# Attention scores over 128 contraction rows, rows cleared by a transfer, and new orders for every engine

## The chip, the cores and the metric

The kernel runs on one core of a Trainium2 chip. The metric is device time of one execution in microseconds (us), taken as the median of repeated runs. Five engines work side by side: PE (TensorE, matrix products), ACT (ScalarE), DVE (VectorE), POOL (GpSimd) and SP (SyncE, which here only issues DMA transfers). They wait for each other through semaphores. SBUF is the on-chip memory with 128 partitions (rows), PSUM holds the results of PE in 8 banks.

## What is computed

Cross attention with 16 heads of 32 columns over 32 batches of 512 queries and 512 keys. The reference, cut to what matters:

```
qn  = layer_norm(q, q_norm_g, q_norm_b);  kvn = layer_norm(kv, kv_norm_g, kv_norm_b)
Q, K, V = (qn @ Wq), (kvn @ Wk), (kvn @ Wv)        # each (32, 512, 512), then 16 heads of 32
scores = einsum('bhqd,bhkd->bhqk', Q, K) / sqrt(32)
attn   = softmax(scores)
ctx    = einsum('bhqk,bhkd->bhqd', attn, V)        # back to (32, 512, 512)
out    = q + gelu(ctx @ Wo + bo)
```

## The kernel before

**Tiling.** The work of a batch is cut into four units, one for each group of four heads (HU = 4, NU = 4); 32 batches give 128 units. Batches 1 to 30 run in one hardware loop, the others are written out. A batch is four steps of each engine's program. In step s the engine does, mixed with each other: the transposed scores, the exponentials and the context of unit s; the plain scores and their maxima of unit s+1; and the projections q and k of unit s+2. So each unit is computed two steps ahead.

**Kinds of work on PE**, by the letters of the ORDER table: `q`, `k`, `v`, `o` are projections, 12 products of 512 columns each, of which one table item issues two (line 856); `x` transposes one token tile (4 short matmuls, line 943); `s` is one plain score product whose row maximum DVE takes (line 883, reader: line 706); `st` is one transposed score product whose exponential ACT takes (line 876, reader: line 563); `pv` is half of a unit's context, 16 narrow matmuls (line 903); `z` sums the probabilities (line 847); `m` transposes the collected maxima (line 965). The two kinds of scores share four PSUM banks in the order in which they are issued.

**The stacks.** A number is kept as a high and a low part. To multiply both at once, the parts of q and k of one unit are stacked over the 128 rows: q_stack and k_stack have two slots each (even and odd units). Rows 0 to 95 hold q high, q high, q low against k high, k low, k high. Rows 96 to 127 of q_stack hold the shift (minus the maximum) that ACT writes once the maxima of the unit are known (line 617); the same rows of k_stack hold constants. The transposed scores contract over all 128 rows, the plain scores, which are needed before a shift exists, over 96 (KROWS).

**How a stack is filled.** ACT writes the high part of a projection, DVE the low part (line 688), and then SP issues three DMAs for q (table item `rq`) and three for k (`rk`), each 256 KB, out of the natural layout into 32 partitions of the stack (`restack`, line 353). Before them SP waits for two things: that the projection has left PSUM, and `stack_used`, which PE raises in the first `pv` that stands behind the last `st` of the step (AFTER_ST), because the unit that is now finished used the same slot. The first `s` of the new unit, in the next step, waits for q_stacked and k_stacked: all six transfers. SP issues everything through one queue, in the order of its table; it also issues the loads of token tiles (`load`), of the residual (`res`, `first_res`) and the stores.

**What sets the order.** Five tables (ORDER), one per engine, each with a string per step. Nothing is scheduled at run time but by semaphores.

Of the kernel before, what the change touches and what calls it, by code (L numbers as in the profile page):

```python
# [9 lines left out]
F32 = mybir.dt.float32  # L10
# [50 lines left out]
    ),  # L61
    "act": (
# [4 lines left out]
    ),  # L67
    "dve": (
# [4 lines left out]
    ),  # L73
    "pool": (
        "ln*3 split add*6 res_add ln*3",
        "ln*2 add*5 res_add add res_add split res_add",
        "split add*6",
        "add split add*5",
    ),
    "sp": (  # L80
        "load*8 rq rk store res",
        "rq rk store res store",
        "store first_res rk rq first_res",
        "rq rk",
# [94 lines left out]
def build(nc, x, ctx_in, q_g, q_b, kv_g, kv_b, wq, wk, wv, wo, bo, out):  # L179
    B = x.shape[0]  # L180
    with ExitStack() as es:
# [6 lines left out]
        def sem(name):  # L188
            return es.enter_context(nc.semaphore(name))
# [58 lines left out]
        stack_used = sem("stack_used")  # L248
        q_stacked = sem("q_stacked")
# [130 lines left out]
        def _(sp):  # L380
            def prepare(b, s):

                if (b, s) == (-1, 1):
# [18 lines left out]
            def batch(b):  # L402
                PLAN = plan_of(b)
                for s in range(NU):
# [4 lines left out]
                    for kind, n, part in PLAN["sp"][s]:  # L409
                        if kind == "load" and valid(b + 1):  # L410
                            load_tile(b + 1, n)
# [580 lines left out]
```

## Time and profile before

| | |
|---|---|
| median of 3 runs | 3265.43 us (3265.21 to 3265.64) |
| the profiled execution | 3262.8 us |
| span of its instructions | 3261.0 us |
| mean granted TensorE clock | 0.998 of full speed |
| PE busy | 99% of the span, 97% of the chain that ended last |
| DVE, ACT, POOL busy | 69%, 70%, 71% |
| DMA engines, mean busy share | 0.6, 105 GB/s |

How to read it: the span is what the records cover; some 2 us lie around it. The chain of work that ended last is followed back from the last instruction; its pieces begin where the piece before ends. Matmuls overlap, so the spacing between their starts, not their durations, is what PE costs.

### The profile page before, as it was taken

To read this page: it belongs to the slowest core of one execution; us is meant where nothing else is said; L and a number is where in the kernel's file an instruction comes from. 1 tells how busy PE (TensorE), PEld (TensorE's weight loads), DVE (VectorE), ACT (ScalarE), POOL (GpSimd) and SP (SyncE) were. 2 spreads that over 40 slices of the span, in tenths; PEclk is the share of its full clock that TensorE was granted. 3 is DMA by queue.
4 is the path that set the end of the run, shared out by engine and by line. 5 is a ranking of instruction groups with operands and counts; after the bars stand their busy time and mean duration, and the time that the engine had idled before them with its cause. 6 is when DMAs were issued, how large, how long until landed. Compare 5 with 4: busy or idle time off the path is not lost.

```text
span 3261.0 us, 49855 instructions
## 1 busy us (share of the span) xinstructions
PE 3230.8 (99%) x16611; PEld 2135.1 (65%) x16611; DVE 2256.9 (69%) x4769; ACT 2280.3 (70%) x3985; POOL 2313.9 (71%) x1544
## 2 busy tenths in 40 slices
PE   8999999999999999999999999999999999999998
PEld 5566666666666666666666666666666666666664
DVE  6667667676676676666766766766667767667664
ACT  5677666777767777667767667776777676677765
POOL 3676776777677767777776677777767776777765
PEclk9999999999999999999999999999999999999999
DMA  5655656566556656565665566665656655666653
GB/s 142 87 108 107 108 104 116 91 111 107 107 104 104 111 107 107 104 118 89 111 109 106 105 102 111 109 104 104 120 86 112 107 107 107 100 111 108 105 79 76
DMA packets 186721, 343.02 MB, mean 105 GB/s; under 512 B 20561, under 2 KB 20577, under 8 KB 186466
## 3 DMA queue, kind: packets, MB, share of 16 engines
q1 hardware_dynamic: 186000, 339.03, 60.0%
q8 instruction: 134, 2.20, 0.3%
q10 hardware_dynamic: 466, 0.80, 0.2%
q14 instruction: 121, 0.99, 0.1%
HBM read 104.87 MB, written 33.55 MB: 42 GB/s over the span
## 4 chain that ended last, share of the span: by engine, by line
PE 97%; DVE 1%; ACT 1%; issue 1%; DMA 0%; POOL 0%; SPq 0%; ACTq 0%; POOLq 0%; DVEq 0%
PE gen L856 43%; PE score L883 16%; PE score L876 15%; PE ctx L903 14%; PE gen L847 4%; PE gen L943 4%; PE gen L965 1%; DVE maxes L706 1%; DMA k_stack<-k_nat 0%; ACT q_stack L617 0%; PE score L788 0%; ACT probs L563 0%; DVE stats L725 0%; PE gen L837 0%; POOL probs L475 0%
## 5 line engine op out<-in xcount | busy, mean ns | idle before, releaser
L475 POOL TENSOR_TENSOR probs<-probs 128x1024 f32<-128x1024 f32 x762 | 1800.3, 2392 | 287.8 <-PE ctx L903 281.6
L706 DVE TENSOR_REDUCE maxes<-score 128x1 f32<-128x512 f32 x2048 | 1294.9, 680 | 217.5 <-PE score L883 213.9
L563 ACT ACTIVATE probs<-score 128x512 f32<-128x512 f32 x2048 | 1090.2, 621 | 141.1 <-PE score L876 137.5
L883 PE MATMUL score<-k_stack,q_stack 96*128 96x512 f32 x2048 | 761.2, 413 | 3.3 <-DVE maxes L706 1.8
L876 PE MATMUL score<-q_stack,k_stack 128*128 128x512 f32 x2048 | 696.4, 406 | 6.6 <-ACT q_stack L617 6.5
L883 PEld LDWEIGHTS score<-k_stack,q_stack 96*128 96x128 f32 x2048 | 378.2, 188 | 221.3 <-ACT probs L563 83.6
L876 PEld LDWEIGHTS score<-q_stack,k_stack 128*128 128x128 f32 x2048 | 374.7, 188 | 199.9 <-DVE maxes L706 64.4
L903 PE MATMUL ctx<-probs,v_sb 128*32 128x512 f32 x4096 | 492.5, 598 | 0.0
L856 PE MATMUL gen<-cT,w_k 128*128 128x512 f32 x1536 | 461.7, 400 | 0.2 <-DVE q_nat L688 0.2
L856 PE MATMUL gen<-w_v,cT 128*128 128x512 f32 x1536 | 461.4, 395 | 0.0
L856 PE MATMUL gen<-xT,w_q 128*128 128x512 f32 x1536 | 447.9, 394 | 0.0
L856 PE MATMUL gen<-w_o,ctx_hl 128*128 128x512 f32 x1488 | 416.4, 396 | 0.0
L491 POOL TENSOR_TENSOR rstd<-var_eps,minus_half 128x1 f32<-128x1 f32 x256 | 140.5, 549 | 335.0 <-DVE neg_mean L737 333.1
L502 POOL TENSOR_TENSOR ctx_hl<-ctx_n,ctx_hl 128x512 fp32r<-128x512 f32 x128 | 164.2, 1283 | 290.4 <-ACT ctx_hl L569 290.4
L617 ACT ACTIVATE q_stack<-max_hl,chunk_mask 32x512 fp32r<-32x512 f32 x512 | 326.3, 706 | 42.3 <-DVE max_hl L771 41.5
L856 PEld LDWEIGHTS gen<-w_v,cT 128*128 128x128 f32 x1536 | 287.3, 189 | 84.1 <-issue 26.8
L856 PEld LDWEIGHTS gen<-xT,w_q 128*128 128x128 f32 x1536 | 288.5, 190 | 60.6
L856 PEld LDWEIGHTS gen<-cT,w_k 128*128 128x128 f32 x1536 | 287.5, 192 | 55.2 <-DVE q_nat L688 1.1
L688 DVE SCALAR_TENSOR_TENSOR k_nat<-gen,bias_k,k_nat 128x512 fp32r<-128x512 f32 x128 | 95.8, 748 | 318.0 <-ACT k_nat L608 318.0
L856 PEld LDWEIGHTS gen<-w_o,ctx_hl 128*128 128x128 f32 x1488 | 276.7, 189 | 57.3
L903 PEld LDWEIGHTS ctx<-probs,v_sb 128*32 128x32 f32 x4096 | 106.9, 109 | 233.8 <-issue 233.8
L574 ACT ACTIVATE v_sb<-gen 128x512 f32<-128x512 f32 x128 | 76.5, 598 | 255.1 <-PE gen L856 255.1
(89 smaller groups left out, 2765.4 us busy)
## 6 DMA issues: line engine op xcount, KB each, us to landing
k_stack<-k_nat SPq DMA_DIRECT2D x384, 256.0 KB, 7.6
q_stack<-q_nat SPq DMA_DIRECT2D x381, 256.0 KB, 5.6
tok<-in_x SPq DMA_DIRECT2D x132, 256.0 KB, 11.0
tok<-in_ctx SPq DMA_DIRECT2D x128, 256.0 KB, 12.0
res<-in_x SPq DMA_DIRECT2D x124, 256.0 KB, 2.7
out<-res SPq DMA_DIRECT2D x124, 256.0 KB, 2.1
probs<-in_L_xattn_Wq SPq DMA_DIRECT2D x1, 1024.0 KB, 8.2
probs<-in_L_xattn_Wk SPq DMA_DIRECT2D x1, 1024.0 KB, 10.4
```

Of the source, the lines that this page charges most:

```text
L475: pool.tensor_tensor(probs[:, c + 1, heads], probs[:, c + 1, heads], probs[:, c, heads], ALU.add).then_inc(pool_added, 1)
L491: pool.tensor_tensor(rstd[:, n:n + 1], var_eps[:, n:n + 1], minus_half[:], ALU.pow).then_inc(ln_rstd, 1)
L502: pool.tensor_tensor(ctx_hl[:, 1, up], ctx_n[:], raw(ctx_hl[:, 0, up]), ALU.subtract).then_inc(ctx_split, 1)
L563: act.activation(probs[:, n, part, :], score_at(s, "st", i)[:], ACT.Exp, scale=SCALE).then_inc(exp_done, 1)
L617: act.activation(q_stack[SROW:P, u1 % 2, :, P * n:P * (n + 1)], raw(max_hl[SROW:P, :]).unsqueeze(1).to_broadcast([SHIFTS, HU, P]), ACT.Ide ...
L706: dve.tensor_reduce(maxes[:, u1 % 2, SROW + i:SROW + i + 1], score_at(s, "s", i)[:], AX_X, ALU.max, negate=True).then_inc(max_done, 1)
L847: mm = pe.matmul(bank[DH * j:DH * (j + 1), :], ones[:, 0:DH], probs[:, c, j, :], start=(i == 0), stop=(i == len(chunks) - 1))
L856: mm = pe.matmul(bank[:, :], stationary(hs, c), moving(hm, c), start=(i == 0), stop=(i == len(TERMS) * NC - 1))
L876: pe.matmul(score_bank(pe, b, s, "st", i)[:, :], k_stack[:, s % 2, part, P * n:P * (n + 1)], q_stack[:, s % 2, part, :], start=True, stop= ...
L883: pe.matmul(score_bank(pe, b, s, "s", i)[:, :], q_stack[0:KROWS, u1 % 2, n, P * part:P * (part + 1)], k_stack[0:KROWS, u1 % 2, n, :], star ...
L903: mm = pe.matmul(ctx_ps[DH * j:DH * (j + 1), :], v_sb[:, c, lo:lo + DH], probs[:, c, j, :], start=(c == 0), stop=(c == NC - 1))
L943: mm = pe.matmul(bank[:, P * c:P * (c + 1)], tok[:, n, P * c:P * (c + 1)], ident[:], start=True, stop=True, is_transpose=True)
```

## The change

There are three parts.

1. **128 rows.** The plain scores (line 883) contract over all 128 rows of both stacks instead of 96. So that rows 96 to 127 add nothing, they are zero in q_stack when the plain scores run. A DRAM tensor zero_rows of 256 KB is filled once from act_out, which is zero at the start. For every unit SP then copies it into rows 96 to 127 of the unit's slot, one DMA of 256 KB, issued with the item `rq`, ahead of the three q transfers, as soon as `stack_used` allows. PE waits for it (`rows_cleared`) at the first `s` of the unit, besides the two waits of before.
2. **Orders.** The tables of all five engines are new. Each step keeps its number of `s`, `st`, `pv`, `q`, `k`, `v`, `x`, `z` and `m`; one item of `o` moves from step 2 to step 0. On DVE and POOL three of the six layer-norm items (`ln`) of step 0 move to step 1, on DVE one `ob` too, on POOL one `res_add`. On SP, `res` and `first_res` items move by up to one step.
3. **One copy.** The copy of the output bias into bias_all on DVE is done at the start of step 0 of batch 0, as the new order no longer begins with `q` there.

```diff
@@ ORDER, step 1 and 2 of "pe" @@
-        "o st*2 o st*3 q st q*4 st q st*3 z x k*3 x st*2 x st k*2 s k st s st*2 pv s x s x s x s pv s x s*2 o*3 "
-        "s*2 x o s o*2 s o s o*2 s o s o*3 m",
+        "st*3 o st q st*3 q*3 st q st q st*2 z x k*2 x k st*2 s k s k st k s st s st x pv x s*4 x pv s x*2 o "
+        "s o s o s*2 o*3 s*2 x o*3 s o*5 m",
...
@@ SP @@
+                    sp.wait_ge(act_out_free, 1)
+                    sp.dma_start(zero_rows.rearrange("r (c n) -> (r c) n", n=D), act_out[:]).then_inc(zeros_stored, 16)
...
+                        if kind == "rq" and valid(b2):
+                            if known(b) and (b, s) == (-1, 2):
+                                sp.wait_ge(zeros_stored, 16)
+                            wait(sp, stack_used, NU * b2 + u2 + 1)
+                            sp.dma_start(raw(q_stack[SROW:P, u2 % 2, :, :]),
+                                         zero_rows.rearrange("r (c n) -> r c n", n=D)).then_inc(rows_cleared[u2 % 2], 16)
                         if kind in ("rq", "rk") and valid(b2) and not (kind == "rq" and known(b) and (b, s) == (-1, 2)):
                             which = kind[1]
                             wait(sp, free[which], NU * b2 + u2 + 1)
-                            wait(sp, stack_used, NU * b2 + u2 + 1)
                             if which == "q":
                                 restack(sp, u2, q_nat, q_stack, ((0, 0), (1, 0), (2, 1)), q_stacked)
                             else:
+                                wait(sp, stack_used, NU * b2 + u2 + 1)
                                 restack(sp, u2, k_nat, k_stack, ((0, 0), (1, 1), (2, 0)), k_stacked)
...
@@ PE @@
                             if i == 0:
                                 wait(pe, q_stacked, 48 * (t1 + 1))
+                                wait(pe, rows_cleared[u1 % 2], 16 * (NU // 2 * b1 + u1 // 2 + 1))
                                 wait(pe, k_stacked, 48 * (t1 + 1))
-                            pe.matmul(score_bank(pe, b, s, "s", i)[:, :], q_stack[0:KROWS, u1 % 2, n, P * part:P * (part + 1)],
-                                      k_stack[0:KROWS, u1 % 2, n, :], start=True, stop=True).then_inc(s_full, 1)
+                            pe.matmul(score_bank(pe, b, s, "s", i)[:, :], q_stack[:, u1 % 2, n, P * part:P * (part + 1)],
+                                      k_stack[:, u1 % 2, n, :], start=True, stop=True).then_inc(s_full, 1)
```

Three places show how the order moves. In square brackets stand the semaphores that an instruction waits for.

SP, the end of step 3: the transfers for unit 1 of the next batch and the token loads behind them. Before:

```order
L353 DMA q_stack<-q_nat 32x4x512 [waits stack_used,q_out_of_psum]
L353 DMA q_stack<-q_nat 32x4x512 x2
L353 DMA k_stack<-k_nat 32x4x512 [waits stack_used,k_out_of_psum]
L353 DMA k_stack<-k_nat 32x4x512 x2
L392 DMA tok<-in_x 128x512 [waits x_in_psum] x4
```

Now:

```order
L422 DMA q_stack<-zero_rows 32x2048 [waits stack_used]
L357 DMA q_stack<-q_nat 32x4x512 [waits q_out_of_psum]
L357 DMA q_stack<-q_nat 32x4x512 x2
L357 DMA k_stack<-k_nat 32x4x512 [waits stack_used,k_out_of_psum]
L357 DMA k_stack<-k_nat 32x4x512 x2
L398 DMA tok<-in_x 128x512 [waits x_in_psum] x4
```

A seventh transfer stands at the head of the six.

PE, from the maxima of unit 2 (line 965, now 978), which end step 1, to the first plain score of unit 3 (the one that waits for the stacks). Before:

```order
L965 MATMUL gen<-ident,maxes 128x128 [waits max_copied,x_out_of_psum]
L856 MATMUL gen<-w_o,ctx_hl 128x512 x8
L883 MATMUL score<-k_stack,q_stack 128x512 [waits max_done,k_stacked,q_stacked]
L856 MATMUL gen<-w_o,ctx_hl 128x512 x2
L883 MATMUL score<-k_stack,q_stack 128x512 [waits max_done]
```

Now:

```order
L978 MATMUL gen<-ident,maxes 128x128 [waits max_copied,x_out_of_psum]
L896 MATMUL score<-k_stack,q_stack 128x512 [waits k_stacked,max_done,rows_cleared1,q_stacked]
L868 MATMUL gen<-w_o,ctx_hl 128x512 x2
L896 MATMUL score<-k_stack,q_stack 128x512 [waits max_done] x3
L868 MATMUL gen<-w_o,ctx_hl 128x512 x2
```

The first plain score stands right behind the maxima; the eight output products that stood between them are behind it or ahead of the maxima.

PE, from the last context half of step 2 to the end of the step. `stack_used` for unit 0 of the next batch was raised by the first context half, ahead of these rows; now the first half stands ahead of the last transposed scores, so that the second half raises it. Before:

```order
L883 MATMUL score<-k_stack,q_stack 128x512 [waits max_done] x2
L856 MATMUL gen<-xT,w_q 128x512 x2
L903 MATMUL ctx<-probs,v_sb 32x512 [waits exp_done]
L903 MATMUL ctx<-probs,v_sb 32x512 x7
L965 MATMUL gen<-ident,maxes 128x128 [waits max_copied,k_out_of_psum]
```

Now:

```order
L896 MATMUL score<-k_stack,q_stack 128x512 [waits max_done]
L896 MATMUL score<-k_stack,q_stack 128x512 [waits exp_done]
L916 MATMUL ctx<-probs,v_sb 32x512 [waits exp_done]
L916 MATMUL ctx<-probs,v_sb 32x512 x7
L868 MATMUL gen<-xT,w_q 128x512 x2
L978 MATMUL gen<-ident,maxes 128x128 [waits max_copied,k_out_of_psum]
```

All plain scores of the step now lie ahead of the context half that raises `stack_used`.

## Rows read from the trace of the kernel before

**Rows 1.** The page: busy time by engine, and the chain that ended last.
```profile
PE 3230.8 (99%) x16611; PEld 2135.1 (65%) x16611; DVE 2256.9 (69%) x4769; ACT 2280.3 (70%) x3985; POOL 2313.9 (71%) x1544
...
PE 97%; DVE 1%; ACT 1%; issue 1%; DMA 0%; POOL 0%; SPq 0%; ACTq 0%; POOLq 0%; DVEq 0%
```
**Rows 2.** Groups by line: both scores; busy us, mean ns, idle before and releasers.
```profile
L883 PE MATMUL score<-k_stack,q_stack 96*128 96x512 f32 x2048 | 761.2, 413 | 3.3 <-DVE maxes L706 1.8 <-DMA k_stack<-k_nat 0.5 <-ACT probs L563 0.4
L876 PE MATMUL score<-q_stack,k_stack 128*128 128x512 f32 x2048 | 696.4, 406 | 6.6 <-ACT q_stack L617 6.5
...
L883 PEld LDWEIGHTS score<-k_stack,q_stack 96*128 96x128 f32 x2048 | 378.2, 188 | 221.3 <-ACT probs L563 83.6 <-issue 52.3 <-DVE maxes L706 14.9
```
**Rows 3.** What SP's queue waited for: us in total, times, longest us.
```profile
SPq L304 <- PE ctx L903: 1443.6, 126, 27.4
```
**Rows 4.** The chain, steps 3 and 0: start us, us, what.
```profile
1540.32 0.45 PE score L876 x2
...
1545.09 1.85 PE ctx L903 x16
1546.95 0.66 PE score L883 x2
1547.60 0.47 PE gen L856 x2
1548.08 0.47 PE score L883 x2
...
1556.02 4.11 PE gen L856 x18
...
1561.49 0.23 PE score L883
```
**Rows 5.** Timeline of SP's queue in the same stretch.
```profile
1546.14 1.85 SPq L353 DMA_DIRECT2D q_stack<-q_nat  x3
1548.09 1.87 SPq L353 DMA_DIRECT2D k_stack<-k_nat  x3
1550.00 2.22 SPq L392 DMA_DIRECT2D tok<-in_x  x4
```
**Rows 6.** The stacks as tiles, same stretch: issues first to last; issue to landing.
```profile
L353 SPq DMA_DIRECT2D q_stack<-q_nat x3: 547/603/612, 1546.1 to 1547.4; - x3
DMA to landing us min/median/max: 4.2/5.6/7.1
L353 SPq DMA_DIRECT2D k_stack<-k_nat x3: 554/612/614, 1548.1 to 1549.3; - x3
DMA to landing us min/median/max: 8.4/9.9/11.0
```
**Rows 7.** Windows with PE: length, PE busy, clock, DMA share, GB/s.
```profile
1553.00:1559.00 6.00, 6.00 (x35) 1.00 1.07 127
1560.50:1565.00 4.50, 4.50 (x24) 1.00 1.04 382
```
**Rows 8.** Steps 0 and 1, unit 2: the chain, and the tile k_stack.
```profile
1576.41 1.85 PE ctx L903 x16
...
1590.70 0.44 PE gen L943 x4
...
1593.21 0.23 PE score L883
...
L353 SPq DMA_DIRECT2D k_stack<-k_nat x3: 548/603/617, 1583.4 to 1584.7; - x3
DMA to landing us min/median/max: 4.4/5.9/7.1
```
**Rows 9.** Steps 1 and 2, unit 3: the same.
```profile
1595.15 1.85 PE ctx L903 x16
...
1612.71 0.23 PE score L883
...
L353 SPq DMA_DIRECT2D k_stack<-k_nat x3: 553/609/614, 1598.1 to 1599.4; - x3
DMA to landing us min/median/max: 8.4/9.9/11.1
```
**Rows 10.** Steps 2 and 3, unit 0: the chain, and the tile q_stack.
```profile
1524.12 1.85 PE ctx L903 x16
...
1544.08 1.01 PE score L883 x3
...
L353 SPq DMA_DIRECT2D q_stack<-q_nat x3: 548/603/616, 1531.6 to 1532.8; - x3
DMA to landing us min/median/max: 4.2/5.6/7.4
```

More of the change, by code:

```diff
@@ L52 @@
     "pe": (
[8 rows of a table removed]
[8 rows of a table added]
     ),
     "act": (
[4 rows of a table removed]
[4 rows of a table added]
     ),
     "dve": (
[4 rows of a table removed]
+        "s*3 ln s q ln s la zt lv la zr ln lv zb s cn la lv s*10 md ml k",
+        "ln ob ln*2 la lv la q zt lv ln la zr la lv zb ln s*2 lv x cn la k s*2 lv x*2 s*2 x*2 s*2 x s*4 x ob "
+        "s*4 x md ob ml",
+        "s*5 ob s*3 zt zr zb s cn s k s*6 md ml q",
+        "k zt zr zb cn s*5 q s*11 md ml",
     ),
     "pool": (
[L75 to L78, printed above, removed]
+        "ln*3 split add*6",
+        "ln*2 res_add ln*2 add ln add*4 res_add add res_add split res_add",
+        "add*6 split",
+        "add*6 split",
     ),
     "sp": (
[L81 to L84, printed above, removed]
+        "load*8 rq rk store",
+        "rq rk res store*2",
+        "res first_res store rk rq",
+        "first_res rq rk",
     ),
@@ L180, in build @@
     B = x.shape[0]
+    zero_rows = nc.dram_tensor("zero_rows", (SHIFTS, HU * D), F32).ap()
     with ExitStack() as es:
@@ L248, in build @@
         stack_used = sem("stack_used")
+        zeros_stored = sem("zeros_stored")
+        rows_cleared = [sem(f"rows_cleared{i}") for i in range(2)]
         q_stacked = sem("q_stacked")
@@ L677, in prepare @@
                     low_weights(3, "o", None)
-                if (b, s) == (0, 0):
-                    dve.wait_ge(bo_mm, 1)
-                    dve.tensor_copy(bias_all[:], ctx_ps[:]).then_inc(bo_ready, 1)
-                    dve.wait_ge(bo_ready, 1)
             def low_part(dst, psum, hi, done, bias=None):
@@ L697, in batch @@
                     t1, t2, tp = NU * b1 + u1, NU * b2 + u2, NU * bp + up
+                    if known(b) and (b, s) == (0, 0):
+                        dve.wait_ge(bo_mm, 1)
+                        dve.tensor_copy(bias_all[:], ctx_ps[:]).then_inc(bo_ready, 1)
+                        dve.wait_ge(bo_ready, 1)
                     for kind, n, part in PLAN["dve"][s]:
```

24 rows, old and new, of the table ORDER are left out of this document.

## The prediction

> **What bounds the kernel now.** I read the page first: PE is busy 99% of the span and makes 97% of the chain that ended last, the other engines stand at 69 to 71% [rows 1]. So only what PE does or waits for can move the time, and with PE this full little is left to gain: both kinds of scores together show 9.9 us of idle time before them, in 4096 matmuls [rows 2]. The next question is which wait is nearly late. SP's queue waited for the context matmuls 126 times, longer than for anything else [rows 3]: each of these is a pair of stacks that may be refilled only when PE raises `stack_used`. That makes a loop: the context half that raises it, then six transfers, then the first plain score of the next step. Its slack is what the change touches, so I measured it for all four units of a batch.
>
> **The slack before.** Unit 1: the context starts at 1545.09 and the first plain score at 1561.49, 16.40 us later [rows 4]. SP issues q from 1546.14, 1.05 us behind the context's start, and k behind it [rows 5]; the last k transfer, issued at 1549.3, lands 11.0 us later, at 1560.3 [rows 6]: 15.2 us after the context. Slack 1.2 us. Unit 2: 16.80 us to the score, the last k issued at 1584.7 lands at 1591.8, slack 1.4 [rows 8]. Unit 3: 17.56 us, landing 1599.4 + 11.1 = 1610.5, slack 2.2 [rows 9]. Unit 0: 19.96 us, landing 1532.8 + 7.4 = 1540.2, slack 3.9 [rows 10]; there q is issued only at 1531.6, because its projection is late.
> Where q and k are issued together, the six are back to back on the DMA engines: q's last lands at 1547.4 + 7.1 = 1554.5, k's at 1560.3, so a stack transfer costs (1560.3 - 1554.5)/3 = 1.95 us of queue [rows 6], the engines' share is over 1.0 meanwhile and they move 127 GB/s [rows 7]. The queue, not the issue (0.6 us each [rows 6]), is the limit. The chain of six from the context's start is 15.3 us.
>
> **Part 2, orders: where the first plain score stands.** I counted in the tables what PE does between the context that raises `stack_used` and the first plain score of the next step, and priced only the difference. Prices from the chain: a pair of products 0.47 or, in a long run, 4.11/9 = 0.46, say 0.465; a score 0.235 [rows 4]; a context half 1.85 [rows 4]; a transposed tile 0.44 [rows 8].
> Unit 1: 2 plain scores and 2 pairs fewer, 1 transposed score more: -1.2 us, so 15.2 us from context to score (was 16.40). As a proof of the prices, the whole stretch of before sums to 16.3: 2 context halves 3.7, 13 plain scores 3.05, 19 pairs 8.85, 2 transposed scores 0.45, the maxima 0.26.
> Unit 2: 1 pair and 1 transposed tile fewer: -0.9, so 15.9.
> Unit 3: 2 plain scores and 3 pairs fewer: -1.85, so 15.7.
> Unit 0: 1 context half, 7 plain scores and 2 pairs fewer: -4.45, so 15.5. Its q projection ends about 2.5 us earlier behind the context than before, so q is issued near 5.0 us, while the k transfers and the new one hold the queue until later: the queue limits here too.
> Total work of PE per batch is the same; it is only put elsewhere. With no new transfer, slack against 15.3 us would be -0.1, +0.6, +0.4 and +0.2, sum 1.1; a weight load of 188 ns [rows 2] must follow the landing before the matmul starts, 4 x 0.19 = 0.75. Left: 0.37 us per batch. The new orders by themselves use up the slack.
>
> **Part 1, the transfer.** It goes out first, at `stack_used`, ahead of all six, so its whole queue time z is added to each of the four chains; nothing covers it, since the slack is gone. Loss per batch: 4z - 0.37. No row shows DRAM to 32 partitions. Below: DRAM to 128 partitions (the token loads) moves 382 GB/s [rows 7], 262 KB in 0.69 us. Above: SBUF to 32 partitions, 1.95 us. Less than 0.69 I exclude, since no stretch moved more. It shares its source with the one and its destination with the other, so I take the middle, 1.32 us. Loss: 4.9 us a batch (2.4 to 7.4). There are 126 such refills [rows 3], so 31.5 batches: 155 us (75 to 234).
> The Trainium skill, "SBUF — State Buffer", section "Door 1: The DMA port swizzle", says that 32 partitions reach only 8 of the 16 ports, 218 GB/s at most. By it 256 KB would take 1.2 us as an estimate and the time would be 3387 us. The trace has no transfer of this kind; the stack transfers into 32 partitions are slower than the rule (127 GB/s).
> The extra wait on PE is one short instruction at the first plain score. Behind it in PE's queue stands everything, so PE idles for the whole loss, and ACT, DVE and POOL only drain meanwhile.
>
> **Part 1, the 128 rows.** Two plain scores cost 0.47, two transposed scores 0.45; a pair of products behind plain scores costs 0.47, in a long run 0.457 [rows 4]. So a 96-row score costs some 10 ns more than a 128-row one, itself and in its wake (0 to 20 by the rounding of the rows). 2048 x 10 ns = 20 us. But time saved between the context and the first plain score is now only waited for; by the tables 39 of 64 plain scores lie in the other stretches. Gain 12 us (0 to 25).
> The Trainium skill, "TensorE: Matmul & The Clock Gate", section "LDWEIGHTS (loading the stationary operand)", holds that columns count and contraction rows don't. By it the gain would be 0 and the time 12 us more than forecast. The weight loads agree (188 ns with 96 rows [rows 2]); the spacing does not.
>
> **Part 2, stalls on PSUM banks.** Two plain scores right behind a context cost 0.66 where others cost 0.47 [rows 4]. I count some 0.7 us of this kind per batch, 22 us in all; a better spread and DVE's lighter step 0 can take some. Only what lies outside the waiting stretches counts: gain 6 us (0 to 22). The `ln`, `res_add`, `ob`, `res` and `first_res` items that move cost nothing: their engines are 30% idle and gain slack when PE waits; if that cover were gone, a late `ln` would cost 0.7 us a batch.
> **Part 3 and the start.** One copy moved, one store of 256 KB ahead of the weight loads: under 1 us, taken as 0.
>
> **Sum.** 155 - 12 - 6 = +137 us. On the profiled execution (span 3261.0, 3262.8 with what lies around it) that is 3400; the median is 2.6 us above the profiled execution: 3402 us.
>
> **Rivals.**
> A, *the full price*: the destination's 32 partitions are what makes a stack transfer slow; z = 1.95, +234 - 18: 3481. For it: both go to 32 partitions. Against: the source is another.
> B, *the cheap price*: the slowness is SBUF as source; z = 0.69, +75 - 18: 3322.
> C, *the transfer is hidden*, the other side: the clearing runs beside the stack transfers, on room that these leave (127 of 382 GB/s [rows 7]). Then z is near 0, the slack just holds, all gains count: 3265 - 20 - 0.5 x 22 = 3234, and it is under 3259 as long as z stays under 0.2 us. Against it: one queue, and a share of 1.0 while it moves 127 GB/s.
> D, *the chain is hidden but DVE is not*: `q` now stands between the plain scores of step 3 on DVE, 0.75 us in a dense run; 24 us lost against gains of 20 to 25: 3265.
>
> **Chances.** Forecast (z near the middle) 0.45, A 0.19, B 0.19, C 0.11, D 0.06. A measurement can tell 0.2%, 6.5 us. Slower 0.83, within 0.05, faster 0.12. Range: 3300 to 3495 holds forecast, A and B with their gains; C and D, 0.17, are left out.
>
> **What would show it.** Right: PE idle of 1 to 2 us at the first plain score of every step, put down to a DMA into q_stack or k_stack, about 5 us a batch; the median landing of k later by z; PE's share near 95%. z itself can be read from the landing of the clearing transfer beside that of the first q. Wrong: k landing no later than 15.3 us behind the context (C), or idle time of PE at the maxima `m` instead (D). If pairs behind plain scores still cost 0.47 at 128 rows, the 12 us fall.

## The result, and the profile after

| | before | after |
|---|---|---|
| median | 3265.32 us (3262.5 to 3265.64, 4 runs) | 3384.74 us (3377.98 to 3393.26, 4 runs) |
| ratio | 1 | 1.0369 (95% interval 1.0345 to 1.0393) |
| span of the profiled execution | 3261.0 us | 3391.5 us |
| mean granted clock of TensorE | 0.998 | 0.991 |

The changed kernel is slower by 119 us. The forecast was 3402 us, the range 3300 to 3495. The profiled execution of after is the longest of the four: it took 3393.26 us, 8.5 us above the median.

The page of after: busy time by engine, then the chain that ended last by engine and by line's group.

```profile
PE 3234.3 (95%) x16611; PEld 2154.9 (64%) x16611; DVE 2262.9 (67%) x4769; ACT 2310.4 (68%) x3985; POOL 2311.0 (68%) x1544
...
PE 54%; DMA 27%; SPq 6%; ACT 5%; DVE 5%; issue 3%; POOL 0%; ACTq 0%; DVEq 0%; POOLq 0%
```

PE does the same 16611 products in the same 3.23 ms, but its share of the chain fell from 97% [rows 1] to 54%. A quarter of the chain is now DMA, with the queue of SP behind it. The groups by line say where PE stood idle (L888 and L896 are lines 876 and 883 of before).

```profile
L888 PE MATMUL score<-q_stack,k_stack 128*128 128x512 f32 x2048 | 711.9, 401 | 4.7 <-ACT q_stack L629 4.5 <-ACT probs L575 0.2
L896 PE MATMUL score<-k_stack,q_stack 128*128 128x512 f32 x2048 | 700.6, 408 | 124.6 <-DMA k_stack<-k_nat 77.4 <-DMA q_stack<-q_nat 42.8 <-ACT probs L575 2.0
```

Idle time of 124.6 us stands before the plain scores, where it was 3.3 us [rows 2], and 120.2 of it was ended by a transfer into a stack. This is the place and the kind of wait that the prediction named.

The waits are not alike in the four units. I measured, over all batches of the loop, how long behind the start of the context half that raises `stack_used` the q and k transfers are issued, the last k (for unit 0 the last q) lands, and the first plain score starts. Medians in us; the last column is the mean of the four scores' sum:

| | unit 1 | unit 2 | unit 3 | unit 0 | sum of scores (mean) |
|---|---|---|---|---|---|
| before: q issued / last landing / score | 1.12 / 15.33 / 16.31 | 1.12 / 15.28 / 16.71 | 1.12 / 15.32 / 17.52 | 7.56 / 15.58 / 19.87 | 70.41 |
| after | 2.55 / 16.78 / 17.04 | 1.44 / 15.80 / 16.05 | 1.44 / 15.70 / 15.95 | 4.70 / 16.61 / 16.66 | 65.99 |

A batch takes 99.8 us before and 103.9 after, on average. The rest of a batch, outside these four stretches, went from 29.4 to 37.9 us: the orders had moved work out of the stretches (8 us), and PE now waits inside them instead of working. The mean wait of PE right before the first plain score is 1.9 us in unit 1, 0.1 in unit 2, 0.45 in unit 3 and 1.4 in unit 0, 3.85 us a batch.

Unit 1 of after is the odd one: its q is issued 1.1 us later than those of units 2 and 3. The queue of SP around it (start us, us, what):

```profile
1611.57 0.32 SPq L422 DMA_DIRECT2D q_stack<-zero_rows  x1
1613.04 1.87 SPq L357 DMA_DIRECT2D q_stack<-q_nat  x3
1615.01 1.86 SPq L357 DMA_DIRECT2D k_stack<-k_nat  x3
```

The clearing leaves at once, then SP waits until 1613.04. What it waits for is on DVE:

```profile
1609.28 3.08 DVE L718 TENSOR_REDUCE maxes<-score 128x1 f32<-128x512 f32 x5 [1.53 <-PE score L896]
1612.28 0.74 DVE L696 SCALAR_TENSOR_TENSOR q_nat<-gen,bias_q,q_nat 128x512 fp32r<-128x512 f32 x1
1612.93 1.28 DVE L718 TENSOR_REDUCE maxes<-score 128x1 f32<-128x512 f32 x2
```

The new table of DVE for step 3 reads `k zt zr zb cn s*5 q s*11`, where the old one had `q s*16`. The low part of q waits behind five maxima, and those wait for five plain scores, which are themselves late. The chain of waits shows the end of it (start us, us, what):

```profile
1616.27 11.00 DMA k_stack<-k_nat
1627.26 0.29 issue
1627.56 0.70 PE score L896 x2
```

Unit 0, in which q comes late and the clearing stands ahead of it:

```profile
1595.56 0.76 DVE q_nat L696
1596.32 0.02 issue
1596.34 0.85 SPq L357
...
1597.88 10.75 DMA q_stack<-q_nat
1608.63 0.04 issue
1608.67 0.51 PE score L896
```

The transfer is issued at 1597.88 and lands 10.75 us later, where a third q transfer of before landed after 7.4 [rows 10].

### The profile page after: what moved, and what is told of

It is laid out like the page before. It is cut to its first block, busy times and chain, and to the rows that moved or that the text cites. A ratio compares the mean times of both kernels' runs of the same rounds, so it can differ in the third digit from the quotient of the medians.

```text
span 3391.5 us, 49985 instructions
## 1 busy us (share of the span) xinstructions
PE 3234.3 (95%) x16611; PEld 2154.9 (64%) x16611; DVE 2262.9 (67%) x4769; ACT 2310.4 (68%) x3985; POOL 2311.0 (68%) x1544
## 4 chain that ended last, share of the span: by engine, by line
PE 54%; DMA 27%; SPq 6%; ACT 5%; DVE 5%; issue 3%; POOL 0%; ACTq 0%; DVEq 0%; POOLq 0%
PE gen L868 20%; DMA k_stack<-k_nat 17%; PE score L896 10%; DMA q_stack<-q_nat 10%; PE ctx L916 9%; PE score L888 8%; SPq L357 6%; DVE maxes L718 3%; ACT probs L575 3%; PE gen L859 3%; PE gen L956 2%; DVE q_nat L696 1%; ACT q_nat L606 1%; ACT L592 1%; ACT act_out L592 0%
## 5 line engine op out<-in xcount | busy, mean ns | idle before, releaser
L896 PE MATMUL score<-k_stack,q_stack 128*128 128x512 f32 x2048 | 700.6, 408 | 124.6 <-DMA k_stack<-k_nat 77.4
L888 PE MATMUL score<-q_stack,k_stack 128*128 128x512 f32 x2048 | 711.9, 401 | 4.7 <-ACT q_stack L629 4.5
L896 PEld LDWEIGHTS score<-k_stack,q_stack 128*128 128x128 f32 x2048 | 377.2, 189 | 353.8 <-issue 136.6
L888 PEld LDWEIGHTS score<-q_stack,k_stack 128*128 128x128 f32 x2048 | 382.6, 189 | 173.3 <-ACT probs L575 60.1
L868 PE MATMUL gen<-w_v,cT 128*128 128x512 f32 x1536 | 450.5, 396 | 0.0
L868 PE MATMUL gen<-cT,w_k 128*128 128x512 f32 x1536 | 432.2, 397 | 0.3 <-DVE q_nat L696 0.3
L625 ACT ACTIVATE max_cut<-gen,cut_sign 32x128 fp32r<-32x128 f32 x128 | 46.0, 359 | 278.1 <-PE gen L978 278.1
```

Of the source, the lines that this page charges most:

```text
L868: mm = pe.matmul(bank[:, :], stationary(hs, c), moving(hm, c), start=(i == 0), stop=(i == len(TERMS) * NC - 1))
L888: pe.matmul(score_bank(pe, b, s, "st", i)[:, :], k_stack[:, s % 2, part, P * n:P * (n + 1)], q_stack[:, s % 2, part, :], start=True, stop= ...
L896: pe.matmul(score_bank(pe, b, s, "s", i)[:, :], q_stack[:, u1 % 2, n, P * part:P * (part + 1)], k_stack[:, u1 % 2, n, :], start=True, stop ...
```

## The experiments

In the experiments "theory" is this account: every microsecond lost is a transfer that lands after the first plain score could start. The medians of before that were taken beside each run lie between 3263.5 and 3265.0 us, so the medians of the runs can be set side by side.

### The two parts, one at a time

First, part 1 with the old tables. The diff against before is the one shown above for SP and PE, without ORDER; the bias copy of part 3 is in it too.

> Part 1 alone: 128 rows and the clearing transfer, with the orders of before. My theory: the old orders leave a slack of 1.0, 1.4, 2.2 and 4.3 us at the first plain score of units 1, 2, 3 and 0; the clearing costs the queue 1.1 to 1.4 us, so only unit 1 waits, about 0.5 us a batch or 15 us, and the 128 rows give back up to 20: 3245 to 3275 us. Rival (the transfer costs its price wherever it stands, as in the changed kernel): the same 120 us as the whole change, 3385.

Measured: 3263.23 us, ratio 0.9996 (0.9986 to 1.0005). With the old orders the clearing costs nothing that can be told. Last landings moved from 15.33, 15.28, 15.32 and 15.58 to medians of 15.73, 15.47, 15.58 and 16.61 us, and the scores, at 16.32, 16.78, 17.50 and 19.80, moved by less than 0.1: the slack of before took it, as its size (1.2 to 3.9 us) had said. The chain of this kernel:

```profile
PE 94%; DMA 2%; DVE 1%; issue 1%; ACT 1%; SPq 1%; POOL 0%; ACTq 0%; POOLq 0%; DVEq 0%
```

Then part 2 alone: the new tables with KROWS and without any clearing.

> Part 2 alone: the new orders with 96 rows and no clearing transfer. My theory: the first plain scores now stand just behind the landing of six transfers, so units 1 and 0 wait a few tenths of a us, 10 to 20 us in all, against up to 22 us of fewer waits for PSUM banks: 3245 to 3280. Rival (the orders themselves are bad, for DVE or ACT): well above 3300 with no DMA in the waits.

Measured: 3318.04 us, 1.0167 (1.015 to 1.0184). Missed, 38 us over the upper end: the orders alone cost 53 us. Their groups by line show 58.3 us of idle time before the plain scores (L884 here), which the profile puts down to "issue", since it saw no releaser:

```profile
L884 PE MATMUL score<-k_stack,q_stack 96*128 96x512 f32 x2048 | 702.5, 409 | 58.3 <-issue 51.6 <-DMA q_stack<-q_nat 3.1 <-DVE maxes L707 0.9
```

By position it is unit 1 alone: q issued at 2.54 us, k landed at 16.77, score at 16.86. Units 2, 3 and 0 start at 15.88, 15.47 and 15.39, where I had predicted 15.9, 15.7 and 15.5 without any wait. Against the 15.2 predicted, unit 1 is 1.66 us late in each batch, 52 us in 31.5 batches. So the waits that the profile puts down to "issue" are waits for a transfer: the score starts 0.09 us behind k's landing.

### The rows

The old tables with 128 rows, and no transfer per unit:

```diff
-                            pe.matmul(score_bank(pe, b, s, "s", i)[:, :], q_stack[0:KROWS, u1 % 2, n, P * part:P * (part + 1)],
-                                      k_stack[0:KROWS, u1 % 2, n, :], start=True, stop=True).then_inc(s_full, 1)
+                            pe.matmul(score_bank(pe, b, s, "s", i)[:, :], q_stack[:, u1 % 2, n, P * part:P * (part + 1)],
+                                      k_stack[:, u1 % 2, n, :], start=True, stop=True).then_inc(s_full, 1)
```

> The row count alone: the plain scores contract over 128 rows with the orders of before; only the first two units have their rows cleared, so the maxima of the later ones take in a former unit's shift. My theory: 10 ns per plain score, 2048 of them: 3245 us (3240 to 3255), with pairs of products behind a plain score at 0.46 instead of 0.47. By the rule that contraction rows don't count (the Trainium skill, TensorE: Matmul & The Clock Gate, section LDWEIGHTS): 3265.

Measured: 3255.95 us, 0.9974 (0.9965 to 0.9984), 8.9 us less than its before. That is 4.3 ns for each of the 2048 products, which are 413 ns long with 96 rows [rows 2] and 412 with 128; their weight loads take 188 ns with either. The same step was taken with the new tables:

> The changed kernel without the clearing transfer, but for the first two units (the maxima of later ones take in a former unit's shift). My theory: the transfer is the whole loss, so this is 120 to 145 us under the changed kernel: 3235 to 3265, and 5 to 20 under the new orders with 96 rows. Rival (a good part of the loss is from the orders or from the clock): over 3300.

Measured: 3309.24 us, 1.0135 (1.012 to 1.015), 8.8 us under the new orders with 96 rows (over the expectation, by the same late q of unit 1: its score stands at 16.85). The rows are worth 9 us in either order. Between this kernel and the changed one lies nothing but the clearing and PE's wait for it: 3384.7 - 3309.2 = 75.5 us.

So the 119 us are the sum of three runs: +53 for the orders, -9 for the rows, +75.5 for the clearing.

### Unit 1's late q

```diff
-        "st*5 k st*11 split q v*2 mh mx*4",
+        "st*5 k st*11 q split v*2 mh mx*4",
...
-        "k zt zr zb cn s*5 q s*11 md ml",
+        "k zt zr zb cn s*2 q s*14 md ml",
```

> The changed kernel with the low part of q earlier in step 3: ACT copies q ahead of the context split, DVE takes it after two plain scores instead of five. Theory 1 (new, from the traces of the changed kernel and of the new orders with 96 rows): in both, unit 1 waits 1.7 us a batch because SP issues its q transfers 2.54 us behind the context instead of 1.12 to 1.44, held by DVE; the clearing hides behind that. With q issued by 1.5 us the chain of unit 1 shrinks from 16.8 to between 15.8 and 16.5: 10 to 35 us less than the changed kernel, 3350 to 3375. Theory 2 (the clearing's price alone binds, as the prediction had it): no change, 3385.

Measured: 3339.75 us, 1.0226 (1.0211 to 1.0241). Two words moved in two tables give back 45 us, more than expected. q of unit 1 is issued at 1.45 us, and its first score starts at 15.70 instead of 17.04, which is 42 us in 31.5 batches. The expectation's sizes were too small because seven transfers behind one another take less time than I gave them (below).

### What the clearing costs

Half the bytes, by clearing half the columns:

```diff
+                                sp.dma_start(raw(q_stack[SROW:P, u2 % 2, 0:HU // 2, :]),
+                                             zero_rows[:, 0:HU // 2 * D].rearrange("r (c n) -> r c n", n=D)).then_inc(rows_cleared[u2 % 2], 16)
```

> The changed kernel with a clearing transfer of half the bytes (heads 0 and 1 only; heads 2 and 3 take in a former unit's shift). If the clearing costs the chains of units 2, 3 and 0 its queue time, 1.1 to 1.3 us whole, and unit 1 nothing (hidden behind the late q), half of it is gone: unit 0 gains 0.6, units 2 and 3 what they wait now, 0.25 and 0.5, so 35 to 45 us under the changed kernel, 3340 to 3350. By the prediction (z on all four chains) 75 us: 3310. If a transfer costs a fixed time whatever its bytes: 3385.

Measured: 3350.65 us, 1.0258 (1.0238 to 1.0277), 34 us less, some 0.45 of 75.5. The cost goes with the bytes. Of the positions, unit 0 moved most (16.66 to 16.04), units 2 and 3 a little (16.05 to 15.90, 15.95 to 15.76), unit 1 not at all (17.04 to 17.03): there the late q hides the clearing.

One part of the cost is not the transfer's. When k lands last and PE waits for it, the first plain score starts 0.09 us behind the landing in the new orders without a clearing, and 0.25 us behind it in the changed kernel. In unit 1 the landing is the same in both (16.77 and 16.78), and only the score moves (16.86 to 17.03). It is the same 0.25 us in the run below in which DVE clears and no transfer does (unit 1: landing 15.34, score 15.58), and what these kernels share is the wait for `rows_cleared` that PE has besides the other two. That is 0.16 us in each of units 1, 2 and 3 when they wait, by this estimate at most 15 us of the 75.5. In unit 0, where q lands last, the score follows within 0.05 us with the added wait and without it. No run has the added wait and nothing else.

The same transfer issued from ACT's queue, with an item `c` in each step of its table, here that of step 3:

```diff
-        "st*5 k st*11 split q v*2 mh mx*4",
+        "st*5 k st*11 split q c v*2 mh mx*4",
...
+                        if kind == "c" and valid(b2):
+                            if known(b) and (b, s) == (-1, 2):
+                                act.wait_ge(zeros_stored, 16)
+                            wait(act, stack_used, NU * b2 + u2 + 1)
+                            act.dma_start(raw(q_stack[SROW:P, u2 % 2, :, :]),
+                                          zero_rows.rearrange("r (c n) -> r c n", n=D)).then_inc(rows_cleared[u2 % 2], 16)
```

> The changed kernel with the clearing issued from ACT's queue, beside the stack transfers instead of ahead of them. My theory: the queues share the same 16 DMA engines, which are full then, so the bytes cost the same: 3365 to 3390. Rival C of the prediction (the stack transfers leave room for another stream): as without clearing, near 3310.

Measured: 3390.65 us, 1.0384 (1.0365 to 1.0402). The bytes cost the other queue's transfers time: in units 2 and 0, where the clearing is issued beside the first stack transfers (1.08 us behind the context), the first of these lands at 6.70 and 6.68 us instead of 5.31. So there is no unused room in which the clearing would be free, and rival C of the prediction, which lived on it, is out.

But that the time is that of the changed kernel hides two effects that cancel. In unit 3 ACT comes to the item only at 2.56 us, behind the issue of q, and the score moves from 15.95 to 16.86. In unit 0 the clearing now goes out ahead of all six transfers instead of between k and q, and the score moves from 16.66 to 15.68, the last landing being 15.57 against 15.37 without any clearing. What a clearing costs depends on its place in the line: the last landing moves by 0.1 to 0.5 us where it leads, in the runs so far, and by 1.2 where it stands in the middle. No run has it at the head in all four units.

The clearing as work of DVE instead of a transfer, with q earlier. In steps 0, 2 and 3 the item `c` stands at the end of DVE's string, in step 1 in its middle:

```diff
-        "ln ob ln*2 la lv la q zt lv ln la zr la lv zb ln s*2 lv x cn la k s*2 lv x*2 s*2 x*2 s*2 x s*4 x ob "
+        "ln ob ln*2 la lv la q zt lv ln la zr la lv zb ln s*2 lv x cn la k s*2 lv x*2 s*2 c x*2 s*2 x s*4 x ob "
...
+                        if kind == "c" and valid(b2):
+                            wait(dve, stack_used, NU * b2 + u2 + 1)
+                            dve.memset(raw(q_stack[SROW:P, u2 % 2, :, :]), 0.0).then_inc(rows_cleared, 1)
```

> No clearing transfer: DVE writes the zeros (one memset of 32x2048 a unit), new orders with q earlier as in e5. My theory: without the transfer the new orders cost 44 us, nearly all of it unit 1's late q (1.6 us a batch, 50 us); with it earlier 3255 to 3270. Rival (the first plain scores stand too early anyway): 3290 to 3310.

Measured: 3302.81 us, 1.0112 (1.0097 to 1.0127). Better than the transfer by 37 us, but 33 us over the upper end of what I expected. The group of the clearing:

```profile
L768 DVE MEMSET q_stack<- 32x2048 f32 x128 | 225.9, 1765 | 58.4 <-issue 58.4
```

1.77 us of DVE at one stroke, in step 1 in the middle of the low parts of x. Units 1, 2 and 0 then start within 0.25 us of the last landing or where no wait is left (15.59, 15.90, 15.39), and unit 3, the one of that step, at 16.63 instead of 15.47, though its k lands at 15.35. These 1.16 us, 37 us in 31.5 batches, account for the miss; a later place for `c` in step 1 was not tried.

### Without any clearing

The stale shift in rows 96 to 127 need not be cleared. It adds one known number to all scores of a query, and the maximum can be put right afterwards. In the old orders:

```diff
                             wait(dve, max_done, 16 * (t1 + 1))
+                            dve.tensor_tensor(maxes[:, u1 % 2, SROW:SROW + SHIFTS // 2],
+                                              maxes[:, u1 % 2, SROW:SROW + SHIFTS // 2],
+                                              maxes[:, u1 % 2, SROW + SHIFTS // 2:P], ALU.add).then_inc(max_corrected, 1)
+                            wait(dve, max_corrected, t1 + 1)
```

> Orders of before, 128 rows, and no transfer per unit. Rows 96 to 127 of q_stack keep the shift of the unit two before (zero only for the first two units, cleared once); since k_stack's constants there hand this shift to every score of a query, the maxima come out too low by it, and DVE adds it back to the 16 collected maxima of a query tile in one extra 128x16 instruction ahead of the copy that PE transposes. Everything is computed. Theory (what the change costs is only what it puts on the path of the stacks; the rows are worth 9 us): the extra instruction, some 0.1 us a unit, is covered because the maxima are ready before PE comes to transpose them: 3256 (3252 to 3261), 0.9955 to 0.9985 of before. Rival: DVE's end of a step is on the path, the instruction with its wait costs 0.15 us x 126 = 19 us: 3268 to 3278.

Measured: 3443.79 us, 1.0558 (1.0544 to 1.0573). Neither theory nor rival: 180 us slower. The profile has 161.6 us of busy time for the added instruction, and the granted clock is 0.983 where the runs of before have 0.995 to 0.998; how the loss divides was not separated. And with the new orders:

> The same, with the orders of the change, except that on ACT step 3 begins `q split` instead of `split q`, and on DVE `q` of step 3 stands behind two plain scores instead of five. Everything is computed. Theory (the new orders lose 53 us only because q of unit 1 is issued 1.4 us late, and 128 rows give back 9): the run of the new orders with 128 rows and no clearing was 3309; less 1.15 to 1.55 us x 31.5 = 36 to 49 for unit 1: 3260 to 3273, level with before or up to 0.25% above or 0.15% below. The first plain score of unit 1 then stands 15.3 to 15.7 us behind its context. Rival: the new orders lose elsewhere too (banks, clock, the extra instruction of DVE), then over 3280.

Measured: 3395.95 us, 1.0415 (1.04 to 1.043). The added instruction as the trace of the first of the two has it, all of its executions, and then one of them beside what POOL did (start us, us, what):

```profile
L778 DVE TENSOR_TENSOR maxes<-maxes x128: 174/642/2290, 58.5 to 3404.5; 128x16 f32<-128x16 f32 x128
```
```profile
1636.19 2.13 DVE L778 TENSOR_TENSOR maxes<-maxes 128x16 f32<-128x16 f32 x1
1638.36 0.17 DVE L782 TENSOR_REDUCE maxes<-maxes 128x16 f32<-128x16 f32 x1
```
```profile
1635.94 7.01 POOL L488 TENSOR_TENSOR probs<-probs 128x1024 f32<-128x1024 f32 x3 [1.95 <-PE ctx L922]
```

Sixteen columns take 174 ns at best and 2290 at worst. In the case shown POOL had begun an addition at 1635.94, the first of three, which ended at 1638.29, and the small instruction of DVE ended at 1638.32, with it. It is so throughout: 127 of the 128 began while POOL was in a two-operand instruction, and each of these ended 0.03 to 0.08 us behind POOL's end. This fits what the Trainium skill, "SBUF — State Buffer", section "Who interferes with whom", states: a DVE instruction with two inputs in SBUF contends with one of GpSimd that reads SBUF. Every other instruction with two tile operands of this kernel's loop on DVE has one of them in PSUM, and no group of those varies by more than 0.04 us between its shortest and its longest.

If that is the cause, the same sum made with one SBUF operand should be free. The row maxima now go into a small tile of their own, unit_max, beside the former shift, and a reduction with add over pairs does it; a second one keeps the new shift there. Against the kernel with the added instruction, the place of the sum:

```diff
-                            dve.tensor_tensor(maxes[:, u1 % 2, SROW:SROW + SHIFTS // 2],
-                                              maxes[:, u1 % 2, SROW:SROW + SHIFTS // 2],
-                                              maxes[:, u1 % 2, SROW + SHIFTS // 2:P], ALU.add).then_inc(max_corrected, 1)
-                            wait(dve, max_corrected, t1 + 1)
-                            dve.tensor_reduce(maxes[:, u1 % 2, SROW + SHIFTS // 2:P],
-                                              maxes[:, u1 % 2, SROW:SROW + SHIFTS // 2].unsqueeze(2), AX_X,
-                                              ALU.max).then_inc(max_copied, 1)
+                            wait(dve, max_kept, t1 - 1)
+                            pair = unit_max[:, u1 % 2, :].rearrange("p (h c) -> p c h", h=2)
+                            dve.tensor_reduce(maxes[:, u1 % 2, SROW:P].rearrange("p (h c) -> p h c", h=2),
+                                              pair.unsqueeze(1).to_broadcast([P, 2, SHIFTS // 2, 2]), AX_X,
+                                              ALU.add).then_inc(max_copied, 1)
```

> As the kernel of the old orders whose DVE adds the former shift back, but without an instruction that reads two operands in SBUF: the row maxima go into a tile of their own beside the former shift, one reduction with add over pairs (one SBUF operand) writes the sums twice into the columns that PE transposes, in place of the copy, and a second small reduction keeps the shift, behind max_hl. Everything is computed. Theory (the added 128x16 tensor_tensor took 1263 ns instead of some 170 because it reads two SBUF operands and waits out POOL's instruction; the Trainium skill, 'SBUF — State Buffer', section 'Who interferes with whom', states such a lock): the reductions take 170 to 250 ns each, and the time is that of the old orders with 128 rows and no transfer, 3256 (3252 to 3262), 0.996 to 0.999 of before. Rival (any further instruction and wait between the last row maximum and PE's transposition costs, since DVE's end of a step is on the path): over 3275.

Measured: 3258.22 us, 0.998 (0.9971 to 0.9989). The 180 us are gone, and this kernel is faster than both: 0.2% under before, 3.7% under the changed kernel. Its two reductions:

```profile
L782 DVE TENSOR_REDUCE maxes<-unit_max 128x32 f32<-128x64 f32 x128 | 28.5, 222 | 4.4
...
L792 DVE TENSOR_REDUCE unit_max<-maxes 128x16 f32<-128x16 f32 x128 | 21.8, 170 | 4.1
```

> The same with the new orders and the earlier q. Everything is computed. Theory (the new orders lose only through q of unit 1, which is earlier here, and through the chain of six transfers that they leave 0.1 to 0.6 us of slack): 3260 to 3273; the first plain scores of units 1, 2, 3 and 0 stand 15.5, 15.9, 15.5 and 15.4 us behind their contexts. Rival (the new orders lose elsewhere too): over 3280.

Measured: 3263.54 us, 0.9994 (0.9985 to 1.0003). First scores at 15.43, 15.90, 15.44 and 15.41 us: within 0.1 us of the theory. So the new orders lose no more than some 5 us against the old ones with the same work (3258.2). They run with the last landing 0.04 to 0.09 us ahead of the score in units 1, 3 and 0, and PE still waits there: 19.3 us before the plain scores, where the old orders have 3.6. On the other side PE itself is busy for 14 us less, as the pages of the two say, first the old orders, then the new:

```profile
PE 3224.9 (99%) x16611; PEld 2126.2 (65%) x16611; DVE 2279.3 (70%) x4898; ACT 2282.3 (70%) x3985; POOL 2316.0 (71%) x1544
```
```profile
PE 3210.7 (98%) x16611; PEld 2144.0 (66%) x16611; DVE 2286.3 (70%) x4898; ACT 2305.1 (71%) x3985; POOL 2313.1 (71%) x1544
```

The new orders do win something, and the waits eat it. The chain of the last kernel shows how near it runs to the transfers:

```profile
PE 85%; DMA 6%; ACT 5%; issue 2%; DVE 1%; SPq 1%; POOL 0%; ACTq 0%; POOLq 0%; DVEq 0%
```

## Why the prediction was right, and where it was not

The time came out 17 us under the forecast and well inside the range. The place and the kind of the loss were the forecast ones: PE waits at the first plain score for transfers into the stacks, 3.85 us a batch where 5 were foretold, and PE is busy 95% of the span. What made up the sum was not: the clearing cost half of its forecast, and new orders that were to gain 6 us lost 53. That the total came within 17 us is luck: these errors cancelled.

**The slack (right).** The orders take 1 to 4 us out of the stretches and leave none but 0.6 us in unit 2. Three of the four positions worked out from the tables were met within 0.25 us, and the last run brought the fourth to 15.43 against 15.2 (there the landing sets it). That the transfer costs only because the slack is gone was shown by the first run, in which it cost nothing. The 0.75 us for weight loads behind the landings was too much: where PE waits for q and k alone, the score starts 0.09 us behind k's landing or 0.04 behind q's, 0.3 us a batch. (Of the prediction's sums one is off by a rounding: (1560.3 - 1554.5)/3 is 1.93, not 1.95.)

**The transfer's own time z (right).** Forecast 1.32 us, between 0.69 and 1.95. The cleanest measure is unit 0, whose q is issued at 4.70 us in either case: its last q transfer lands at 15.37 us behind the context without a clearing ahead of it, at 16.00 with half a clearing and at 16.61 with a whole one, so z = 1.24. By the rate for 32 partitions in the Trainium skill, "SBUF — State Buffer", section "Door 1: The DMA port swizzle", the prediction's estimate was 1.2, and this trace agrees. A and B are both out: a transfer from DRAM into 32 partitions costs neither the 1.95 us of a stack transfer nor the 0.69 of a token load. What makes a stack transfer slower was not separated; besides its source, its packets differ (2 KB against 8 KB).

**z on each of the four chains (wrong).** The step was "z is added to each of the four chains", 155 us net. Measured: 75.5. In unit 1 the late q hid it, in units 2 and 3 it cost 0.2 to 0.5 us, because the transfers behind it ran faster, and only in unit 0 the whole of it showed (15.39 to 16.66). Together the four scores moved by 2.1 us, 66 us in 31.5 batches. "The extra wait on PE is one short instruction" put at nothing what shows as 0.16 us in three of the four units.

**The orders' own loss (missed), and rival D.** D said that `q` between the plain scores of DVE would cost 24 us of DVE's time against equal gains. The place was right, but what is late is not DVE: it is SP behind it, by 1.4 us, and all six transfers behind SP. The step that failed is "With no new transfer, slack against 15.3 us would be -0.1" in unit 1: the 15.3 held only for q issued 1.05 us behind the context. The price of the orders was 53 us, and it stood beside the forecast, not in place of it.

**The rows (mis-sized).** 12 us forecast by 10 ns a score, 8.9 measured by 4.3 ns. The differences in the chain's rows, 0.47 against 0.45 and 0.46, were near their rounding; 0 to 25 was the honest range. The Trainium skill, "TensorE: Matmul & The Clock Gate", section "LDWEIGHTS (loading the stationary operand)", says of the weight load that its columns count and not its contraction rows. For the load this case agrees (188 ns with 96 rows and with 128). Carried over to the whole product, as the prediction did, it would have been 9 us wrong. Why the product with 96 rows costs more stays open.

**The banks (not refuted).** 6 us of gain, up to 22, were taken for fewer stalls. PE's busy time in the profiles falls by 12 us from the old to the new orders with 96 rows (3230.8 to 3218.7) and by 14 in the last pair of runs, so a gain of this size is there; but that it comes from the PSUM banks was not shown, and it is less than the waits that the orders bring.

**The clock (missed).** Behind some of the waits the granted clock of TensorE falls, which no step priced. Windows of PE in after (length, busy, clock, DMA share, GB/s):

```profile
1612.00:1625.00 13.00, 13.00 (x67) 1.00 0.96 135
1625.00:1628.00 3.00, 1.11 (x5) 1.00 1.07 227
1628.00:1633.00 5.00, 5.00 (x17) 0.66 0.81 300
1633.00:1640.00 7.00, 7.00 (x42) 1.00 0.00 1
```

PE was busy for only 1.11 of the 3 us up to 1628, then part of the next 5 us ran at the lower level, 1.2 GHz of 2.4, and 17 instructions went through them where the rows around show five or six a us. Over the whole span the clock of 0.991 against 0.998 is 3391.5 x 0.009 - 3261.0 x 0.002 = 24 us of full-speed time against the waits that it follows; the part of it in which PE would have waited anyway costs nothing, so 24 is a bound above. The fall is not bound to each wait. Between 150 and 3200 us there are ten such stretches in the changed kernel, two without the clearing and none with the clearing and the early q. In that last one PE's busy time is 19 us less (3215.0 against 3234.3), of which the clock makes up 3391.5 x 0.009 - 3336.4 x 0.004 = 17 by the same count.

In numbers: forecast 155 - 12 - 6 = 137; measured 75.5 - 9 + 53 = 119.5, each from the medians of a pair of runs and so with the clock that its waits bring. The clearing was 80 us too dear, the rows 3 us too generous, the orders 59 us too cheap: 137 - 80 + 3 + 59 = 119.

## What to carry to other kernels

Before a table of orders is tightened around a chain of transfers, measure the slack of that chain, and check every instruction ahead of the first issue on every engine that it waits for: one small operand that moved behind five others on DVE cost more than the work that was rearranged. An added transfer cost least at the head of its line here. A bandwidth that was free in one order is not free in another, so cost such a transfer together with the order that it will run in. And where a buffer must be cleared only so that its content adds nothing, ask first if what it adds can be subtracted from a small result.

## What the runs showed of the hardware

**Stack transfers that queue directly behind the clearing are faster.** In before, the stack transfers of unit 1 land one by one every 2.06 us (5.31, 7.36, 9.43, 11.47, 13.55, and the last at 15.33 us behind the context). From the first landing to the fifth their packets of 2 KB take 270 ns each on average, and the engines move 128 GB/s. In the run with the clearing and the early q, where the clearing's packets of 8 KB go just ahead, they land every 1.85 to 1.95 us (6.49, 8.34, 10.19, 12.04, 13.98, and the last at 15.45); the packets take 244 ns, at 143 GB/s. So seven transfers end 0.1 us behind six. It is so in unit 0 too when ACT's queue sends the clearing first (6.68, 8.48, 10.28). They do not speed up where the clearing goes between k and q (unit 0 of after: 12.75, 14.81) or where q is issued 1.5 us behind it (unit 1 of after: 2.06 us apart), and hardly behind half a clearing (unit 3: 5.81, 7.80, 9.83). Packet size, source and amount all differ between the clearing and a stack transfer, and what causes this was not tried.

**An added wait on PE** shows as 0.16 us: the first plain score starts 0.09 us behind k's landing with two waits before it and 0.25 us with three.

**Two operands in SBUF on DVE** cost 1263 ns on average for 128x16, with POOL in a two-operand instruction of its own at the start of 127 of 128, where a reduction of the same size takes 170; the same sum by reduction takes 222.

**96 rows against 128**: the product with fewer rows is not the faster one. It costs 4.3 ns more each in the time of the kernel, in both orders (3264.9 to 3255.95 and 3318.0 to 3309.2 us).
